# Attention of the first stage: normalising after the values product instead of before the transposes

## The reference

```python
xn = _ln(x, g_x, b_x); ln = _ln(latents, g_l, b_l)
q = ln @ w_q
kv_in = jnp.concatenate([xn, ln], axis=1)
k, v = jnp.split(kv_in @ w_kv, 2, axis=-1)
q, k, v = (split(q) * scale, split(k), split(v))
sim = jnp.einsum('bhid,bhjd->bhij', q, k)
attn = jax.nn.softmax(sim, axis=-1)
out = jnp.einsum('bhij,bhjd->bhid', attn, v)
out = out.transpose(0, 2, 1, 3).reshape(B, Lq, H * DH)
return _ln(out @ w_out, g_o, b_o)
```

## Time and profile before

| What | Value |
|---|---|
| median of 3 runs | 2225.14 us (2224.73 to 2228.25) |
| span of the profiled execution | 2225.1 us |
| PE busy | 2186.7 us, 98% |
| PEld busy | 1865.5 us, 84% |
| DVE busy | 1728.1 us, 78% |
| ACT busy | 1282.0 us, 58% |
| POOL busy | 645.1 us, 29% |
| DMA packets | 111642, 129.57 MB |

### The profile page before, as it was taken

The page is one execution under the profiler, slowest core; times in us unless marked ns, Lnnn a source line. Parts: engine busy times, 40 slices in busy tenths (PEclk is TensorE's granted clock), DMA queues, the critical chain, the costliest instruction groups (busy, mean ns, idle before and its releaser), DMA issues. The chain is left out here.

```text
span 2225.1 us, 48355 instructions
## 1 busy us (share of the span) xinstructions
PE 2186.7 (98%) x15486; PEld 1865.5 (84%) x15486; DVE 1728.1 (78%) x6112; ACT 1282.0 (58%) x3251; POOL 645.1 (29%) x1162
## 2 busy tenths in 40 slices
PE   8999999999999999999999999999999999999997
PEld 6777777777777777777699999999878888888886
DVE  6788888888888888888675555555579999999986
ACT  6776776776776776776443333433345555555553
POOL 1123223222232232232220000000355555555541
PEclk9999999999999999999899999999999999999999
DMA  5320110110110110110052222221212222222210
GB/s 189 124 97 22 37 40 23 37 39 21 40 38 20 39 39 20 40 32 27 11 161 73 81 86 72 81 77 41 89 58 65 65 65 64 65 65 65 65 39 20
DMA packets 111642, 129.57 MB, mean 58 GB/s; under 512 B 14898, under 2 KB 98089, under 8 KB 111264
## 3 DMA queue, kind: packets, MB, share of 16 engines
q1 hardware_dynamic: 98249, 105.06, 14.9%
q0 software_dynamic: 12288, 21.21, 3.3%
q10 hardware_dynamic: 855, 0.19, 0.0%
HBM read 84.26 MB, written 54.53 MB: 62 GB/s over the span
## 5 line engine op out<-in xcount | busy, mean ns | idle before, releaser
L711 ACT ACTIVATE a_prob<-a_prob,a_nmax 128x376 f32<-128x376 f32 x512 | 309.7, 606 | 155.3 <-DVE a_nmax L857 155.3
L1457 ACT ACTIVATE e_hidden<-e_first,keep_b 128x256 f32<-128x256 f32 x320 | 134.1, 471 | 283.3 <-PE e_first L80 282.8
L857 DVE CUSTOM_DVE_ANT_0 a_prob<-a_score,a_mask_row 128x376 f32<-128x376 f32 x512 | 266.6, 540 | 10.8 <-issue 5.6
L80 PE MATMUL e_second<-e_w,e_hidden 128*128 128x256 f32 x1920 | 239.5, 284 | 0.0
L80 PEld LDWEIGHTS e_second<-e_w,e_hidden 128*128 128x128 f32 x1920 | 232.6, 192 | 0.0
L869 DVE TENSOR_SCALAR a_prob<-a_prob,a_rden 128x376 f32<-128x376 f32 x512 | 220.9, 453 | 2.5
L1151 PE MATMUL a_turned<-keep_ident,a_prob 128*128 128x128 f32 (+1 forms) x1536 | 217.3, 277 | 2.8 <-DVE a_probT L876 1.6
L1151 PEld LDWEIGHTS a_turned<-keep_ident,a_prob 128*128 128x128 f32 (+1 forms) x1536 | 173.5, 142 | 43.5 <-issue 27.6
L1142 PE MATMUL a_score<-a_kT,a_qT 64*128 64x376 f32 x1024 | 196.4, 502 | 0.0
L876 DVE COPY a_probT<-a_turned 128x384 f32<-128x384 f32 x256 | 139.8, 546 | 54.4 <-PE a_turned L1151 54.4
L719 ACT ACTIVATE a_probT<-a_turned 128x384 f32<-128x384 f32 x256 | 124.9, 488 | 92.1 <-PE a_turned L1151 91.7
(11 more groups left out here) (237 smaller groups left out, 5231.1 us busy)
## 6 DMA issues: line engine op xcount, KB each, us to landing
w_in<-W SPq DMA_DIRECT2D x32, 512.0 KB, 4.1
slots<-a_zeros SPq DMA_DIRECT2D x8, 1280.0 KB, 8.7
keep_rows<-slots SPq DMA_DIRECT2D x40, 256.0 KB, 3.9
answers<-e_y SPq DMA_DIRECT2D x40, 256.0 KB, 2.2
a_xn<-x SPq DMA_DIRECT2D x32, 256.0 KB, 2.9
a_xr<-x SPq DMA_DIRECT2D x32, 256.0 KB, 3.8
x<-r_x SPq DMA_DIRECT2D x32, 256.0 KB, 4.0
w_in<-x SPq DMA_DIRECT2D x32, 256.0 KB, 2.6
```

The costliest lines, as they stand in the source:

```text
L80: last = nc.tensor.matmul(out, stationary(a, t), moving(b, t), start=start and n == 0, stop=stop and n == len(todo) - 1)
L711: nc.scalar.activation(prob[:, u % 4, a], prob[:, u % 4, a], ACT.Exp, bias=nmax[:, u % 4, a:a + 1], scale=-1.0, accum_out=den[:, u % 4, a: ...
L857: nc.vector.tensor_tensor_reduce(prob[:, u % 4, a], score[SCORE_AT[u][a]][:, 0:NKV], mask_row[:, p], -1.0, 3.0e38, ALU.add, ALU.min, nmax[ ...
L1457: nc.scalar.activation(hidden[:, 2 * j + i], first[:, j, i * CH:(i + 1) * CH], ACT.Relu, bias=b1[:, 2 * j + i, bass.ds(e, 1)]).then_inc(re ...
```

## The change

`normalise` is gone. `turn_prob` transposes the exponentials as they are, and waits for `exp_ok` instead of `norm_ok`. `over_sum` runs once per pair (4 columns at a time instead of 2). The row sums belong to queries, which after the values product lie along the columns, so the reciprocals have to lie along the columns too, the same in all 64 rows of a head. SP does that in a new `spread_shares`, per pair: it waits for `rden`, stores 128 x 4 floats as rows into a new array `shares` in the chip's memory, waits until they have landed, and issues two loads that repeat a row of 256 over 64 partitions each, into `share`. DVE `attended` multiplies the bank of the values product by `share` into a new tile `att`; that alone frees the bank (`att_ok`, in place of `att_lo`, in all of PE's waits but `output`'s and `router_turn`'s and `router_logits`' in step B + 1). `att_high` and `att_low` read `att` instead of the bank.

Cut to its core:

```diff
-        rden = sb("a_rden", [P, 4, 2])
+        rden = sb("a_rden", [P, 2, 2, 2])
+        share = sb("a_share", [P, KI, S])
+        att = sb("a_att", [P, KI, S])
...
+            def spread_shares(b, m):
+
+                done = KI * b + m
+                eng.wait_ge(rden_ok, done + 1)
+                at_least(eng, share_in, 32 * (done - KI + 1))
+                eng.dma_start(t["shares"][m].rearrange("i a q -> q (i a)"),
+                              rden[:, m % 2].rearrange("p i a -> p (i a)"),
+                              allow_slow_non_contiguous=True).then_inc(share_out, 16)
+                eng.wait_ge(share_out, 16 * (done + 1))
+                at_least(eng, att_ok, done - KI + 1)
+                for a in range(2):
+                    eng.dma_start(share[64 * a:64 * a + 64, m].rearrange("p (i q) -> p i q", i=QT),
+                                  t["shares"][m, :, a].partition_broadcast(64)) \
+                        .then_inc(share_in, 16)
...
                 if here(s - 4):
                     store(eng, s - 4, p)
+                if live(s - 2):
+                    spread_shares(s - 2, 1)
+                    spread_shares(s - 2, 2)
+                    spread_shares(s - 2, 3)
                 if live(s + 2):
                     load(s + 2, p)
+                if live(s - 1):
+                    spread_shares(s - 1, 0)
...
             def att_high(b, m):
-                eng.wait_ge(pv_made, KI * b + m + 1)
+                eng.wait_ge(att_ok, KI * b + m + 1)
                 at_least(eng, out_ok, b)
-                nc.scalar.activation(att2[:, 0, m], (bank_a if m == 1 else bank_b)[:, 0:S], ACT.Copy).then_inc(att_hi, 1)
+                nc.scalar.activation(att2[:, 0, m], att[:, m], ACT.Copy).then_inc(att_hi, 1)
...
-            def over_sum(b, u):
+            def over_sum(b, m):
+
                 for a in range(2):
-                    eng.wait_ge(exp_ok[a], NG * b + u + 1)
-                nc.vector.reciprocal(rden[:, u % 4], den[:, u % 4]).then_inc(rden_ok, 1)
-
-            def normalise(b, u, a):
-
-                eng.wait_ge(rden_ok, NG * b + u + 1)
-                nc.vector.tensor_scalar(prob[:, u % 4, a], prob[:, u % 4, a], rden[:, u % 4, a:a + 1], None, ALU.mult) \
-                    .then_inc(norm_ok[a], 1)
+                    eng.wait_ge(exp_ok[a], NG * b + 2 * m + 2)
+                at_least(eng, share_out, 16 * (KI * b + m - 1))
+                nc.vector.reciprocal(rden[:, m % 2], den[:, m % 2 * 2:m % 2 * 2 + 2]).then_inc(rden_ok, 1)
...
+            def attended(b, m):
+
+                eng.wait_ge(pv_made, KI * b + m + 1)
+                eng.wait_ge(share_in, 32 * (KI * b + m + 1))
+                at_least(eng, att_lo, KI * (b - 1) + m + 1)
+                nc.vector.tensor_tensor(att[:, m], (bank_a if m == 1 else bank_b)[:, 0:S], share[:, m],
+                                        ALU.mult).then_inc(att_ok, 1)
...
                 else:
-                    eng.wait_ge(att_lo, KI * b)
+                    eng.wait_ge(att_ok, KI * b)
                 _, lo, hi = VALUE_ROWS[j]
...
                 for a in range(2):
-                    eng.wait_ge(norm_ok[a], NG * b + u + 1)
+                    eng.wait_ge(exp_ok[a], NG * b + u + 1)
                     at_least(eng, prob_ok[a], NG * b + u)
```

More of the change, by code:

```diff
@@ L738, in step @@
                     nc.scalar.activation(wo[:, 0], stage_o, ACT.Copy).then_inc(w_high, 1)
+                if live(s - 2):
+                    turned_out(s - 2, 1, 0)
                 if live(s - 3):
@@ L741, in step @@
                 if live(s - 2):
-                    turned_out(s - 2, 1, 0)
                     exps(s - 2, 4, 1)
@@ L928, in step @@
                     weights_lower(3, wo[:], stage_o)
-                if live(s - 2):
-                    normalise(s - 2, 2, 0)
                 if live(s - 3):
-                    att_low(s - 3, 3)
+                    attended(s - 3, 3)
                 if live(s - 2):
@@ L937, in step @@
                     choose(eng, s - 4, 0)
+                if live(s - 3):
+                    att_low(s - 3, 3)
+                if here(s - 4):
+                    choose(eng, s - 4, 1)
                 if live(s - 2):
                     row_max(s - 2, p, 5, 1)
[L940 to L941 removed]
                 if isinstance(s, int) and s == B + 2:
                     w1_lower(1)
[L944 to L945 removed]
                 if here(s - 4):
@@ L954, in step @@
                 if live(s - 2):
-                    normalise(s - 2, 3, 0)
+                    over_sum(s - 2, 1)
                 if here(s - 4):
                     choose(eng, s - 4, 4)
-                if live(s - 2):
-                    normalise(s - 2, 3, 1)
+                if live(s - 1) and not (isinstance(s, int) and s == 1):
+                    kvin_low(s - 1, q, 0)
                 if here(s - 4):
@@ L980, in step @@
                     row_max(s - 2, p, 6, 1)
-                    over_sum(s - 2, 4)
-                    normalise(s - 2, 4, 0)
-                    normalise(s - 2, 4, 1)
-                    att_low(s - 2, 0)
+                    over_sum(s - 2, 2)
+                    attended(s - 2, 0)
                     turned_out(s - 2, 3, 1)
                     row_max(s - 2, p, 7, 0)
+                    att_low(s - 2, 0)
                     row_max(s - 2, p, 7, 1)
@@ L1016, in step @@
                 if live(s - 2):
-                    normalise(s - 2, 6, 1)
+                    attended(s - 2, 1)
                 if routed(s - 4):
@@ L1044, in step @@
                     row_max(s - 1, q, 3, 0)
-                    normalise(s - 1, 0, 0)
-                    normalise(s - 1, 0, 1)
+                if live(s - 2):
+                    att_low(s - 2, 2)
+                if live(s - 1):
                     row_max(s - 1, q, 3, 1)
```

77 lines of the change are left out of this document (28 added, 49 removed).

## The result

| | median | range | runs | against before |
|---|---|---|---|---|
| before | 2226.69 us | 2224.73 to 2228.95 | 4 | |
| changed | 2727.47 us | 2720.81 to 2736.34 | 4 | 1.225, 95% interval 1.2224 to 1.2277 |

The account below looks back on a forecast made before the run. The prediction took PE, busy 200 of 200 us in steady steps of 33.58 us, as the bound. From 2225.1 us, less 1.5 at the start, plus 0.5 at the end, it forecast 2224.1 us, no change, range 2219.5 to 2230.

Parts of the forecast that it names:

- the detour as a latency: Reciprocals through memory per pair: 9.4 us, between 5.8 and 17.6, fits the 12.7 us allowed before `output`; no cost.
- the three rows: Landings in the trace used for the detour: 2.2 us quickest median, 4.0 for the x1 store, 8.1 at the start.
- Cost nothing: SP's queue: transfers behind a spread move by some microseconds but are used a step or more later; no cost.
- rival 1: Detour misses its deadline at pair 3, DVE blocked, then `output`; about 31 us per microsecond beyond 12.7, up to 2376 us; 0.07.
- `output`'s slack there: Head of the step: second half of `att2` ends at about 503.7, leaving 0.5 us of 2.0 before `output`; no wait.
- DVE's work is worth nothing: Steady steps: DVE loses 6.2 us per step, some 200 us over 32 batches, hidden by PE's 33.58 us step.
- Start: Start of the stage: PE's waits of 0.96 and 0.23 us go, that of 1.18 loses 0.3; together 1.5 us gained.
- End: End of the stage: PE's wait for `att2` before the last `output` grows by one multiplication, say 0.5 us.
- Rival 2: PE's modelled busy time hides waits that a lighter DVE takes out: 7.4 us less, 2216.7 us; chance 0.04.
- Rival 3: Steps 1 to 3: stores of zeros delay first detours, 2.7 us late, 8.1 us over three batches, 2232 us; chance 0.12.
- Rival 4: End of the stage: sooner transposes close idle time, PE's clock stays up; 4.9 us less, 2219.2 us; chance 0.05.

Follow-up runs that it names:

- g1_no_wait_both: Changed kernel with both routing pieces put back, slow store kept, SP not waiting for it, loads from a row of ones (no division): 2292.37 us, ratio 1.0291.
- h1_4B_apart: Changed kernel with both routing pieces put back, pieces touching, SP waiting, loads from a row of ones elsewhere (no division): 2607.05 us, ratio 1.1713.
- f4_order_both: Changed kernel, detour and store as they are, with `choose` 7 and `counts_in` put back: 2724.89 us, ratio 1.2239.
- f1_no_detour_both: Changed kernel without the detour (`share` holds ones, so no division), both routing pieces put back: 2228.82 us, ratio 1.0008.
- f3_64B_both: Changed kernel with both routing pieces put back, pieces stored 64 bytes apart, SP waiting, loads from a row of ones (no division): 2228.87 us, ratio 1.0003.
- f2_16B_both: Whole change with both routing pieces put back, store in 128 pieces of 16 bytes, two multiplications per pair: 2234.3 us, ratio 1.0034.

## Why the prediction was wrong, point by point

**The step that failed: the detour as a latency.** The prediction asked whether one pair's reciprocals reach DVE in 12.7 us, took 4.0 us for the store's landing from a store of 256 KB, and 8.1 us as its upper end. It then put the detour's cost at nothing. Two things were wrong with it.

- *The size.* The store takes 10.0 us until its loads go out, above the upper end. None of the three rows was a store in pieces of 4 bytes. The loads were sized about right: 0.96 for their issue and 4.0 for their landing against a median of 4.9 for both. A bracket from the nearest rows bounds only what is of the same kind, and here nothing was.
- *The sum that was not made.* SP waits for each store before it issues anything, four times in a step. "Cost nothing" for SP's queue looked at what stands behind a spread, and not at how long SP is occupied per step. With the prediction's own values that sum is 4 x (0.48 + 4.0 + 0.96), 21.8 us, under 33.6; with its upper end it is 38.2 us, already over. With what was measured it is 49.4. By the latency rule of rival 1 the measured detour, 10.0 + 4.9 = 14.9 us from the store's issue to the multiplication, would cost 2.2 x 31 = 68 us, and with the longest 11.4 us of the loads in every step 270 us; the occupancy gives 490 of the 501. Rival 1 had the place right in part (DVE blocked at the multiplication, PE behind it, though pair 1 waits longest, 7.2 us in the median against 4.4 for pair 3), and neither price nor mechanism.

The runs divide the detour, with both routing pieces put back: 66 us are the slow stores without SP's wait (g1_no_wait_both over its before), 314 more come with SP's wait (h1_4B_apart, 380 us over its before, less 66), and 118 more in f4_order_both, whose loads read the stretch that is being written (with the reservation made above).

The prediction weighed the Trainium skill against this term (DMA: Bandwidth & Descriptors, section Rules for kernel authors): a last dimension that isn't contiguous becomes one descriptor per element. The trace agrees. The page of the profile after counts 86,578 packets under 512 bytes, 71,680 more than before; 128 stores of 512 make 65,536 of them. The estimate from that page's section Bandwidth in the Trainium skill, 0.34 us at 10.5 ns a packet, took the figure as one engine's own, which the section, written of loads, doesn't say; counted over all 512 packets it would be an estimate of 5.4 us. Neither gives the 10.0 us measured: the engines were done by 612.3 us and SP went on at 619.57. The same page of the Trainium skill, section Specifications, says that transfers under 512 bytes are read, modified and written. By that alone pieces 16 and 64 bytes apart should be as slow as touching ones; at 2.81 and 2.12 us they aren't, so the measurement decides that the distance matters.

**A step that was missing: two routing pieces.** The prediction showed DVE's new order at the head of the step and checked `output`'s slack there. It didn't walk through the rest of the step, where `choose` 7 had passed behind `out_stat` and `counts_in` behind `out_centre`. Both feed PE within a microsecond or two. Alone in the kernel before they cost 1.46% and 0.66%; in the change they are 1.4% that the detour covers. That PE's instructions and their order stay was true, and that a step can only change by what PE waits for too. The list of what PE waits for left out the routing.

**What held.** With detour and routing pieces taken out, f1_no_detour_both is the change as the prediction saw it: 1.0008 of before, interval 0.9997 to 1.0018, no change. Its window from 400 to 600 us, and PE at the places of the earlier trace rows:

```profile
400.00:600.00 200.00, 200.00 (x1422) 155.85 (x1422) 144.02 (x597) 144.01 (x393) 56.42 (x102) 1.00 0.11 33
```
```profile
65.21 1.66 PE L80 MATMUL a_work<-a_wkv,a_kvin 128*128 128x512 f32 x6 [0.98 <-DVE a_att L886]
...
1107.59 4.83 PE L80 MATMUL keep_bank<-a_wo,a_att 128*128 128x256 f32 x24 [1.57 <-DVE r_lsum L275]
```

- *DVE's work is worth nothing.* DVE lost 24 us of 168 in that window, PE stays at 200 of 200. 36 us were forecast; why it is less wasn't traced.
- *Start.* The waits for `normalise` and at 57.10 are gone, as forecast; the third fell from 1.18 to 0.98 us (0.9 forecast). Together 1.4 us for 1.5.
- *End.* `output` waits 1.57 us instead of 1.09: 0.48 us for a forecast of 0.5. The forecast sum of 1 us is less than the runs can tell.
- *Rival 2* (a lighter DVE takes hidden waits out of PE) is out: from the `output` at 503.85 to the last one it takes 603.7 us, before 603.0, and 0.5 of that is the end's wait.
- *Rival 3* (stores of zeros) is seen at DVE and not in the time. Where the stores of `share` are quick, as in f3_64B_both, DVE waits at the place that the rival named, batch 0's pair 1 (first line below), 1.75 us for a worst case of 2.7. No other multiplication there waits half a microsecond for its loads, PE has no wait from it, and the time is that of before. PE's waits at the start of f2_16B_both, 0.63 and 1.63 us where before had 0.23 and 1.18, fit another reason better: DVE's multiplications there waited for PE or for nothing, not for a load, and take 1.24 us in their two pieces instead of 0.42 (second line: the one before the first of these waits).

```profile
49.10 0.42 DVE L910 TENSOR_TENSOR a_att<-keep_bank,a_share 128x256 f32<-128x256 f32 x1 [1.75 <-DMA a_share<-ones]
```
```profile
54.73 1.24 DVE L905 TENSOR_TENSOR a_att<-a_work,a_share 64x256 f32<-64x256 f32 x2 [0.93 <-PE a_work L1191]
```

- *Rival 4* (the clock stays up at the end) did not come: the last `output` takes 4.83 us, still far from 3.00, and the granted clock from 1096 to 1098 us is 0.50 as before.

## What to carry to other kernels

When a queue's engine is made to wait for its own transfer, add up its waiting over a whole step, beside asking whether each transfer meets its deadline: taken alone, a detour of 14.9 us misses its deadline of 12.7 by little, but four waits of 10 us, with the issuing between them, came to 49.4 us in a step of 33.6. When a change rewrites an engine's order, follow every instruction that another engine waits for past each instruction that itself waits, also in parts that have nothing to do with the change; one late piece hides the next, so mend and measure one at a time. And a store in pieces of 4 bytes wants a layout in which a partition writes its few floats side by side, or in which the pieces don't touch.

## What the runs showed of the hardware

- 512 pieces of 4 bytes stored side by side take 8.9 to 10.0 us (medians of three runs and the change) from issue to the next instruction that waits for them; the same pieces 16, 64 and 512 bytes apart take 2.81, 2.12 and 1.85 us, and the same 2 KB as 128 pieces of 16 bytes 1.53 us. In the window looked at, the DMA engines were done 1.9 us after the store's issue, and SP went on 7.3 us after that; what fills that time isn't shown.
- Such a store holds up others: where SP didn't wait for it, the loads of x landed after 10.2 us (median of 32) instead of 3.0 beside quick stores, and the stores still cost 66 us.
- Where the loads read the stretch being written, each of these stores took about 0.9 us longer (10.0 for 9.1 us, means of 128, one run each); that the loads are the reason isn't shown.
